# Input quarters of an attention unit rounded to two halves three steps ahead of their mixing instead of one

## The chip, the cores and the metric

One core of a Trainium2 chip runs the whole program. The metric is the device time of one execution in microseconds (us). A measurement is a median over runs.

## What is computed

The reference is a small tower: a token mixing, causal linear attention with its MLP, and a routed expert layer. The change touches the first part only, where the mixing of the input meets the attention:

```python
h = einsum('bhid,oi,od->bho', x, weighted_sum, weight)     # 16 sequences x 512 rows x 256
x0 = layernorm(h); hn = layernorm(x0) * g1 + beta1
q, k = phi((hn @ wq) @ proj), phi((hn @ wk) @ proj)        # 16 heads of 64
v = hn @ wv
# causal: kv += k v^T, ksum += k; out = q kv / (q ksum + 1e-6)
x1 = x0 + out @ wo                                         # then MLP, then the routed experts
```

## The kernel before, in words

**Precision.** Every float32 operand of a matmul is carried as two float16 tiles, a high part (rounded) and a low part (the rest), and each product is three matmuls (`three`, lines 541 to 545). So each operand needs one rounding and one subtraction. For the input the rounding to `xh` is ScalarE's (`split`, line 719) and the subtraction into `xl` is GpSimd's (line 959), each on a 128x512 tile. For the features phi(q) and phi(k), VectorE adds up `z` (line 869) and casts it to `hi` (line 874), and GpSimd makes `lo` (line 965).

**Units and steps.** The attention phase works in 32 units of 256 tokens, two for each of 16 sequences. h is 0 for the first unit of a sequence and 1 for the second. A unit has eight steps, s0 to s7 (`unit`, lines 382 to 439); each step reads out one group of four heads (`outputs`), turns an earlier group (`turn`), makes scores for a group two steps ahead (`scores`), and beside that does a piece of dense work: the eight features (n0 to n7) and four value tiles of the next unit, and the projection of the last one. Features sit at s0 (n0), s1 (n1, n2), s2 (n3), s4 (n4), s5 (n5, n6), s6 (n7). The unit after next gets its first normalisation at s0 to s2 (`mean`, `var`, `rstd`, `x0`, `normed`), and the unit three ahead is mixed at s4 to s7, one of four input quarters each (`mixed`, lines 352 to 357), with 12 matmuls for a quarter.

**Order.** One function, `run`, writes the same order of steps out for every engine, and each engine takes those steps that it has a part in, strictly in that order. What belongs to a step on an engine waits on semaphores of the others. SyncE's queue (SP) is part of this: at `split` of a quarter it waits until `xh` and `xl` of that quarter are made (lines 481, 482) and then loads the quarter of the following unit into the freed buffer (line 483, 256 KB); at `phi` of a feature it waits for `hi` and `lo` and moves them to where the scores read them: eight DMAs for a feature of q (n even), four for one of k (n odd), lines 507 to 519. The scores of s0 (line 628) wait until n7 has been moved.

**Where the change bites.** The quarter k is split at step s3 + k, so `xh` and `xl` for a mixing are made one step ahead of it. `mixed(u, k)` issues the mixing of k and then the split of k + 1. In `unit`, the split stands after `scores_split` and `sums_split` and ahead of the late feature's `phi`, so on VectorE's and GpSimd's side it stands between `kvl` (line 984) and the next `lo`. The buffers `xh` and `xl` have a place of their own for each of the four quarters, and their owner waits only for the mixing of the same quarter one unit earlier.

Of the kernel before, what the change touches and what calls it, by code (L numbers as in the profile page):

```python
# [28 lines left out]
XS = XK // 2  # L29
# [35 lines left out]
def after(u, n):  # L65

    return u[0] + (u[1] + n) // 2, (u[1] + n) % 2
# [27 lines left out]
def attention_phase(nc, io, w1_w, w2_w, mlp_loaded):  # L95
# [4 lines left out]
    with ExitStack() as ctx:  # L100
# [223 lines left out]
        def run(engine, steps):  # L324


            def step(name, *args):
                if name in steps:
                    steps[name](*args)

            def use(u, what, bank, before):


                kind, n = what
                if kind == "p":
                    step("project", after(u, -1), bank, before)
                elif kind == "f":
                    step("features", after(u, 1), n, bank, before)
                else:
                    step("values", after(u, 1), n, bank, before)  # L340

            def finish(u, what, bank):
                if what[0] == "f":
                    step("phi", after(u, 1), what[1], bank)
                elif what[0] == "p":
                    step("project_read", after(u, -1), bank)
                    step("residual", after(u, -1))

            def real(u):
                return u[0] < SEQS  # L350

            def mixed(u, k):
                step("mix", u, k)
                if k < XS - 1:
                    step("split", u, k + 1)
                else:
                    step("h", u)

            def normed(u):
                step("mean", u)  # L360
                step("centre", u)
                step("var", u)
                step("rstd", u)
                step("x0", u)
                step("normed", u)

            def dense(turn, first, last):


                slots, n = [], turn % 2  # L370
                before = {n: ("v", VALS - 2, 1), 1 - n: ("v", VALS - 1, 1)}
                for s in range(8):
                    uses = [], []
                    for place, (kind, k) in enumerate(DENSE[s]):
                        if not ((kind == "p" and first) or (kind != "p" and last)):
                            uses[place].append(((kind, k), n % 2, before[n % 2]))
                            before[n % 2] = (kind, k, 0)
                        n += 1
                    slots.append(uses)
                return slots  # L380

            def unit(u, start=False, last=False):


                i, h = u
                slots = dense(h, start, last)
                ahead, far = after(u, 2), after(u, 3)
                for s in range(8):
                    c, g = 2 * h + s // 4, s % 4
                    early, late = slots[s]  # L390

                    summed = (c, g - 2) if g >= 2 and c < CH - 1 else (c - 1, g + 2) if g < 2 and c > 0 else None

                    if g < 2:
                        quad = (i, c, g + 2)
                    elif c < CH - 1:
                        quad = (i, c + 1, g - 2)
                    else:
                        quad = None if last else (i + 1, 0, g - 2)
                    if s == 2 and real(ahead):  # L400
                        step("x0", ahead)
                        step("normed", ahead)
                    for what in early:
                        use(u, *what)
                    step("outputs", i, c, g)

                    if g >= 2:
                        step("turn", i, c, g - 2)
                    elif c > 0:
                        step("turn", i, c - 1, g + 2)  # L410
                    elif not start:
                        step("turn", i - 1, CH - 1, g + 2)
                    for what in early:
                        finish(u, *what[:2])
                    if quad is not None:
                        step("scores", *quad)
                    step("outputs_split", i, c, g)
                    if s == 1 and real(ahead):
                        step("var", ahead)
                        step("rstd", ahead)  # L420
                    for what in late:
                        use(u, *what)
                    if summed is not None:
                        step("sums", i, *summed)
                    if g in (1, 2) and c < CH - 1:
                        step("keys", i, c, g - 1)
                    if quad is not None:
                        step("scores_split", *quad)
                    if summed is not None:
                        step("sums_split", i, *summed)  # L430
                    if s == 0 and real(ahead):
                        step("mean", ahead)
                        step("centre", ahead)
                    if s == 3 and real(far):
                        step("split", far, 0)
                    if s >= 4 and real(far):
                        mixed(far, s - 4)
                    for what in late:
                        finish(u, *what[:2])

            step("split", (0, 0), 0)
            for k in range(XS):
                mixed((0, 0), k)
            normed((0, 0))
            step("split", (0, 1), 0)
            slots = dense(-1, True, False)
            for s in range(8):
                for what, bank_no, before in slots[s][0] + slots[s][1]:
                    use((0, -1), what, bank_no, before)
                    finish((0, -1), what, bank_no)  # L450
                if s < XS:
                    mixed((0, 1), s)
                elif s == 4:
                    normed((0, 1))
            step("split", (1, 0), 0)
            for k in range(XS):
                mixed((1, 0), k)
            for q in range(2):
                step("scores", 0, 0, q)
                step("scores_split", 0, 0, q)  # L460
            unit((0, 0), start=True)
            unit((0, 1))
            for i in range(1, SEQS - 1):
                unit((i, 0))
                unit((i, 1))
            unit((SEQS - 1, 0))
            unit((SEQS - 1, 1), last=True)
            step("turn", SEQS - 1, CH - 1, 2)
            step("turn", SEQS - 1, CH - 1, 3)
            step("project", (SEQS - 1, 1), LAST_BANK, ("p", 0, 1))  # L470
            step("project_read", (SEQS - 1, 1), LAST_BANK)
            step("residual", (SEQS - 1, 1))
# [4 lines left out]
        def _(sp):  # L477
# [53 lines left out]
            for k in range(XS):  # L531
                load((0, 0), k)
            run(sp, dict(split=split, phi=phi, residual=residual))
            sp.wait_ge(x1_stored, 16 * UNITS)
            sp.wait_ge(hx_stored, 16 * UNITS)
# [4 lines left out]
        def _(pe):  # L540
# [147 lines left out]
            def turn(i, c, g):  # L688
# [6 lines left out]
                for part, src in enumerate((oh, ol)):  # L695
                    for f in range(2):
                        w = 2 * part + f
                        mm = pe.transpose(pT[:, w * P:(w + 1) * P], src[:, n % 2, f * P:(f + 1) * P], ident[:, :])  # L698
                mm.then_inc(turned, 1)

            run(pe, dict(mix=mix, mean=mean, var=var, features=features, values=values, scores=scores, keys=keys,
                         outputs=outputs, sums=sums, turn=turn, project=project))

        @block.scalar
        def _(act):
# [109 lines left out]
            def sums_split(i, c, g):  # L815
# [5 lines left out]
                                     ACT.Copy).then_inc(kvh_ready, 1)  # L821

            run(act, dict(outputs=outputs, split=split, h=h, centre=centre, rstd=rstd, normed=normed, features=features, values=values,
                          scores_split=scores_split, turn=turn, outputs_split=outputs_split,
                          sums_split=sums_split))
# [1365 lines left out]
```

## Time and profile before

| what | us |
|---|---|
| median of three runs | 2545.34 |
| lowest, highest run | 2538.14, 2553.37 |
| the profiled execution, device time | 2542.18 |
| its span, first to last instruction | 2540.4 |

Of the span, TensorE is busy 2215.7 us, VectorE 1784.6, ScalarE 1524.6 and GpSimd 1467.8. The attention phase runs from about 45 to 1550 us; after it come the MLP and the routed phase, which the change does not touch and which begin when the attention phase is over. In the tables PE is TensorE, DVE VectorE, ACT ScalarE, POOL GpSimd, and SPq the queue of SyncE. The span given in a row of a timeline is start, duration, engine, line, operation, and in brackets how long the engine sat idle before it and what released it.

### The profile page before, as it was taken

Reading aid. Unit: us, or ns where it says so; the run is one execution under the profiler, and the core shown is the slowest. Engines: PE = TensorE matmul, PEld = TensorE weight load, DVE = VectorE, ACT = ScalarE, POOL = GpSimd, SP = SyncE. Lnnn points to the kernel's source line nnn. Section 1 sums busy time; section 2 is a strip of 40 time slices with the busy share of each in tenths; the row PEclk is TensorE's granted clock in tenths of the full one; section 3 lists DMA queues with packets and bytes.
Section 4 is the critical chain, followed back from the end, with each engine's and each line's share of the span. In section 5 each row is a group of like instructions: output and inputs, shape, how many; then the busy total and the mean of one; then the engine's idle time right before and its main releaser. Section 6 shows DMA issues by size and latency. Waiting matters only on the chain. (4 is left out here: it accounts for less than half of the span.)

```text
span 2540.4 us, 64867 instructions
## 1 busy us (share of the span) xinstructions
PE 2215.7 (87%) x24112; PEld 1732.1 (68%) x24112; DVE 1784.6 (70%) x3983; ACT 1524.6 (60%) x2890; POOL 1467.8 (58%) x1449
## 2 busy tenths in 40 slices
PE   3799999999989899999999986799999999994764
PEld 2577777778778777777778775466666666662653
DVE  3477777777777777777777775478788887874443
ACT  3476676676766676667667664556566565651322
POOL 1466666575666666656657654035646555556676
PEclk8899999999999999999999998899999999997897
DMA  3344444344454343434433333111212111100775
GB/s 112 97 119 113 122 123 124 104 131 122 105 132 124 100 105 102 108 99 105 110 101 104 89 87 112 40 60 45 82 43 83 45 60 52 40 22 22 166 139 72
DMA packets 323208, 236.43 MB, mean 93 GB/s; under 512 B 40345, under 2 KB 288141, under 8 KB 322896
## 3 DMA queue, kind: packets, MB, share of 16 engines
q1 hardware_dynamic: 286640, 197.30, 28.6%
q0 software_dynamic: 23808, 21.74, 4.9%
q10 hardware_dynamic: 12448, 13.24, 1.6%
q8 instruction: 195, 3.19, 0.5%
q14 instruction: 117, 0.96, 0.1%
HBM read 73.32 MB, written 82.58 MB: 61 GB/s over the span
## 5 line engine op out<-in xcount | busy, mean ns | idle before, releaser
L965 POOL TENSOR_TENSOR lo<-z,hi 128x512 f16<-128x512 f32 x256 | 306.1, 1196 | 342.8 <-DVE hi L874 328.5
L1850 POOL DMA_INDIRECT slot_dram<-xt,slot_u x256 | 267.0, 1043 | 77.4 <-issue 77.4
L543 PE MATMUL pF<-nh,qk_h 128*128 128x256 f16 x1024 | 282.7, 276 | 7.5 <-DVE nl L862 4.4
L545 PE MATMUL pF<-nl,qk_h 128*128 128x256 f16 x1024 | 282.6, 276 | 0.0
L544 PE MATMUL pF<-nh,qk_l 128*128 128x256 f16 x1024 | 282.6, 276 | 0.0
L789 ACT ACTIVATE sh<-sm 128x512 f16<-128x512 f32 x256 | 159.5, 623 | 106.3 <-DVE sm L895 106.2
L984 POOL TENSOR_TENSOR kvl<-kvacc,kvh 128x260 f16<-128x260 f32 x192 | 157.4, 820 | 77.2 <-ACT kvh L820 77.1
L869 DVE SCALAR_TENSOR_TENSOR z<-pF,z 128x512 f32<-128x512 f32 x256 | 174.9, 683 | 24.6 <-ACT z L772 22.2
L768 ACT ACTIVATE z<-pF 128x512 f32<-128x512 f32 x256 | 150.4, 587 | 69.6 <-PE pF L545 69.6
L543 PE MATMUL pM<-xh,tok_h 128*128 128x256 f16 x512 | 141.3, 276 | 53.9 <-POOL xl L959 53.3
L895 DVE TENSOR_TENSOR sm<-pS,mask 128x512 f32<-128x512 f32 x256 | 174.5, 681 | 17.2 <-PE pS L629 16.9
L977 POOL TENSOR_TENSOR ol<-on,oh 128x256 f16<-128x256 f32 x256 | 171.9, 672 | 24.4 <-ACT oh L812 24.4
L874 DVE CAST hi<-z 128x512 f16<-128x512 f32 x256 | 174.7, 682 | 8.8
L543 PE MATMUL pO<-vh,sh 128*128 128x65 f16 x1024 | 120.5, 194 | 57.1 <-issue 48.2
L796 ACT ACTIVATE ot<-pT 128x512 f16<-128x512 f16 x256 | 149.3, 583 | 33.1 <-PE pT L698 32.9
L628 PE MATMUL pS<-qdh,ks 128*128 128x128 f16 x1024 | 143.6, 221 | 29.1 <-DMA ks<-lo 28.2
L772 ACT ACTIVATE z<-z 128x512 f32<-128x512 f32 x256 | 161.4, 630 | 8.1
L812 ACT ACTIVATE oh<-on 128x256 f16<-128x256 f32 x256 | 105.5, 412 | 96.9 <-DVE on L927 94.0
L1838 POOL TENSOR_TENSOR xt<-xn,xt 128x512 f16<-128x512 f32 x32 | 40.0, 1269 | 208.5 <-ACT xt L1521 208.5
L2100 POOL DMA_INDIRECT out_rows<-yb,xg x80 | 126.7, 1583 | 58.3 <-ACT yb L2045 33.0
L919 DVE TENSOR_SCALAR dn<-pO 128x4 f32<-128x4 f32 x256 | 39.9, 156 | 170.0 <-PE pO L545 169.7
L959 POOL TENSOR_TENSOR xl<-w_w,xh 128x512 f16<-128x512 f32 x128 | 147.9, 1158 | 18.1 <-ACT xh L719 18.1
(298 smaller groups left out, 8494.2 us busy)
## 6 DMA issues: line engine op xcount, KB each, us to landing
w_w<-in_x SPq DMA_DIRECT2D x128, 256.0 KB, 3.0
qdh<-hi SPq DMA_DIRECT2D x512, 64.0 KB, 2.1
qdl<-lo SPq DMA_DIRECT2D x512, 64.0 KB, 2.1
ks<-hi SPq DMA_DIRECT2D x256, 64.0 KB, 2.1
ks<-lo SPq DMA_DIRECT2D x256, 64.0 KB, 2.1
slot_dram<-blank ACTq DMA_DIRECT2D x8, 1360.0 KB, 7.1
xg<-slot_dram SPq DMA_DIRECT2D x40, 272.0 KB, 3.2
x_dram<-x SPq DMA_DIRECT2D x32, 256.0 KB, 2.4
```

Of the source, the lines that this page charges most:

```text
L543: pe.matmul(out, wh, mh, start=first, stop=False, skip_group_check=True)
L544: pe.matmul(out, wl, mh, start=False, stop=False, skip_group_check=True)
L545: return pe.matmul(out, wh, ml, start=False, stop=last, skip_group_check=True)
L772: nc.scalar.activation(z[:, s, :, :], z[:, s, :, :], ACT.Exp, scale=-1.0, bias=-math.log(PHI_DOWN)).then_inc(e_ready, 1)
L789: nc.scalar.activation(sh[:, q, :, :], sm[:, n % 2, :, :], ACT.Copy).then_inc(sh_ready, 1)
L869: nc.vector.scalar_tensor_tensor(z[:, s, :, :], pF[bank_no][:, :].rearrange("p (b n) -> p b n", b=2), 0.0, z[:, s, :, :], ALU.max, ALU.add ...
L874: nc.vector.tensor_copy(hi[:, n % MOVES, :, :], z[:, s, :, :]).then_inc(fh_ready, 1)
L895: nc.vector.tensor_tensor(sm[:, n % 2, :, :], pS[:, :].rearrange("p (a b) -> p a b", b=P), mask[:, :].unsqueeze(1).broadcast_to([P, 4, P]) ...
L965: nc.gpsimd.tensor_tensor(lo[:, n % 2, :, :], z[:, units(w, FEATS, n) % ZS, :, :], hi[:, n % MOVES, :, :], ALU.subtract).then_inc(fl_ready, 1)
L977: nc.gpsimd.tensor_tensor(ol[:, n % 2, :], on[:, n % 2, :, :].rearrange("p a b -> p (a b)"), oh[:, n % 2, :], ALU.subtract).then_inc(ol_re ...
L984: nc.gpsimd.tensor_tensor(kvl[:, heads, :], kvacc[:, heads, :], kvh[:, heads, :], ALU.subtract).then_inc(kvl_ready, 1)
L1850: nc.gpsimd.indirect_dma_start(io["slot_dram"], bass.IndirectOffsetOnAxis(slot_u[:, i % XT, c, k:k + 1], 0), xt[:, i % XT, c, :], None, bo ...
```

## The change

All four splits of a unit move: in the steady units from s3, s4, s5, s6 to s1, s2, s3, s4. The mixings stay at s4 to s7. For the first units, which are written out by hand, the splits of unit (0, 1) are issued together ahead of its mixing; those of (0, 0) and (1, 0) keep their order.

```diff
             def mixed(u, k):
                 step("mix", u, k)
-                if k < XS - 1:
-                    step("split", u, k + 1)
-                else:
+                if k == XS - 1:
                     step("h", u)
...
-                    if s == 3 and real(far):
-                        step("split", far, 0)
+                    if 1 <= s <= XS and real(far):
+                        step("split", far, s - 1)
                     if s >= 4 and real(far):
                         mixed(far, s - 4)
...
-            step("split", (0, 0), 0)
             for k in range(XS):
+                step("split", (0, 0), k)
                 mixed((0, 0), k)
             normed((0, 0))
-            step("split", (0, 1), 0)
+            for k in range(XS):
+                step("split", (0, 1), k)
...
-            step("split", (1, 0), 0)
             for k in range(XS):
+                step("split", (1, 0), k)
                 mixed((1, 0), k)
```

## Rows read from the trace of the kernel before

**Rows 1.** The page: span and busy time of each engine.
```profile
span 2540.4 us, 64867 instructions
PE 2215.7 (87%) x24112; PEld 1732.1 (68%) x24112; DVE 1784.6 (70%) x3983; ACT 1524.6 (60%) x2890; POOL 1467.8 (58%) x1449
```

**Rows 2.** TensorE's waits, 200 to 1450 us: total, times, longest.
```profile
PE pO L543 <- issue: 41.1, 27, 1.8
PE pM L543 <- POOL xl L959: 33.6, 55, 1.9
PE pS L628 <- DMA ks<-lo: 23.4, 24, 2.6
```

**Rows 3.** Timeline of ScalarE: the first and last `h` of 28 steady units.
```profile
157.12 0.60 ACT L725 ACTIVATE hT<-pM 128x512 f32<-128x512 f32 x1
...
1451.28 0.60 ACT L725 ACTIVATE hT<-pM 128x512 f32<-128x512 f32 x1
```

**Rows 4.** Timeline of TensorE: mixing at s7, outputs at s4, scores at s0 twice.
```profile
753.51 0.27 PE L543 MATMUL pM<-xh,tok_h 128*128 128x256 f16 x1 [1.19 <-POOL xl L959]
...
782.26 0.19 PE L543 MATMUL pO<-vh,sh 128*128 128x65 f16 x1 [1.63 <-issue]
...
1408.22 0.22 PE L628 MATMUL pS<-qdh,ks 128*128 128x128 f16 x1 [1.60 <-DMA ks<-lo]
...
1497.85 0.27 PE L628 MATMUL pS<-qdh,ks 128*128 128x128 f16 x1 [2.48 <-DMA ks<-lo]
```

**Rows 5.** Timeline of VectorE: casts of n4, with loads behind them and without.
```profile
1387.21 0.43 DVE L874 CAST hi<-z 128x512 f16<-128x512 f32 x1
...
1479.33 0.43 DVE L874 CAST hi<-z 128x512 f16<-128x512 f32 x1
```

**Rows 6.** Timeline of SyncE's queue from n4's first move to n7's last.
```profile
1387.66 0.59 SPq L507 DMA_DIRECT2D qdh<-hi  x1
...
1397.12 0.54 SPq L483 DMA_DIRECT2D w_w<-in_x  x1
1397.70 0.59 SPq L507 DMA_DIRECT2D qdh<-hi  x1
...
1400.29 1.63 SPq L516 DMA_DIRECT2D qdl<-lo  x1
...
1405.22 1.25 SPq L519 DMA_DIRECT2D ks<-lo  x2
```

**Rows 7.** The same queue at s5 of a unit where it runs dry.
```profile
470.03 1.25 SPq L519 DMA_DIRECT2D ks<-lo  x2
472.20 0.33 SPq L483 DMA_DIRECT2D w_w<-in_x  x1
```

**Rows 8.** Timeline of ScalarE at s1: h = 1 (720 us), h = 0 (767 us).
```profile
721.16 0.40 ACT L820 ACTIVATE kvh<-kvacc 128x260 f16<-128x260 f32 x1
...
767.51 0.61 ACT L789 ACTIVATE sh<-sm 128x512 f16<-128x512 f32 x1
771.90 0.91 ACT L754 ACTIVATE nh<-w_w,b 128x256 f16<-128x256 f32 x2 [3.78 <-DVE w_w L856]
```

**Rows 9.** Timeline of GpSimd: s1 of h = 1, s1 of h = 0, s5.
```profile
721.64 0.88 POOL L984 TENSOR_TENSOR kvl<-kvacc,kvh 128x260 f16<-128x260 f32 x1 [1.79 <-ACT kvh L820]
...
770.05 1.47 POOL L965 TENSOR_TENSOR lo<-z,hi 128x512 f16<-128x512 f32 x1 [3.35 <-DVE hi L874]
...
792.82 1.15 POOL L959 TENSOR_TENSOR xl<-w_w,xh 128x512 f16<-128x512 f32 x1
```

**Rows 10.** Timeline of VectorE: cast n2 (h = 1, h = 0), n6; `nl`, `sl`.
```profile
722.61 0.43 DVE L874 CAST hi<-z 128x512 f16<-128x512 f32 x1
...
769.48 0.43 DVE L874 CAST hi<-z 128x512 f16<-128x512 f32 x1
...
772.51 0.88 DVE L862 SCALAR_TENSOR_TENSOR nl<-w_w,b,nh 128x256 f16<-128x256 f32 x2 [0.31 <-ACT nh L754]
...
781.37 0.68 DVE L902 TENSOR_TENSOR sl<-sm,sh 128x512 f16<-128x512 f32 x1
...
791.29 1.02 DVE L902 TENSOR_TENSOR sl<-sm,sh 128x512 f16<-128x512 f32 x1
...
792.95 1.30 DVE L874 CAST hi<-z 128x512 f16<-128x512 f32 x1
```

**Rows 11.** Timeline of TensorE: a mixing of unit (0, 1).
```profile
77.70 0.27 PE L543 MATMUL pM<-xh,tok_h 128*128 128x256 f16 x1 [2.73 <-POOL xl L959]
```

## The prediction

> **What bounds the kernel now.** I read the page first [rows 1]: TensorE is busy for 87% of the span, which invites the thought that any stall taken from it is gained. TensorE's waits come next [rows 2]. In 27 units (200 to 1450 us) it waits 33.6 us for `xl`, the wait that the change aims at: 1.24 us a unit, mostly at the mixing of s7, as in [rows 4], 753.51. But it also waits 23.4 us for the last move of `ks` (0.87 a unit, at the scores of s0) and 41.1 us at the outputs of s4, where the row names no releaser; there `sl`, made by VectorE just before, ends the wait [rows 4, 10]. A wait that stands right behind the removed one takes back what it gives, so the question is what sets the time of the scores of s0.
>
> The steady unit lasts (1451.28 - 157.12) / 28 = 46.2 us [rows 3]. I cut it at two events: the cast of n4 at s4, and the scores of s0.
>
> Second part, n4's cast to s0's scores. In the unit of 1387 us the cast ends at 1387.64 and SyncE's queue begins n4's moves at 1387.66 [rows 5, 6]. From there it issues back to back: 24 moves (n4 to n7: 8 + 4 + 8 + 4), each 0.59 to 0.65 us from start to start, and two loads of input quarters, each 0.58 us to the next start (1397.12 to 1397.70). Its last move ends at 1406.47 and the scores start 1.75 later, having waited 1.60 us [rows 4, 6]. So the queue, not TensorE, ends this part: 20.58 us. A few issues take 1.0 to 2.0 us instead of 0.61 (1.63 at 1400.29), about 1.3 us extra in a unit; I see no link with the loads. The trace holds its own experiment: in the unit of 1479 us there is neither load nor mixing; cast end 1479.76, scores 1497.85, so 18.09 us, and TensorE waits even longer, 2.48 us [rows 4, 5]. With no mixing at all in the way, the scores still wait for the queue.
>
> First part, s0's scores to n4's cast, about 25.6 us. TensorE makes `mean`, then ScalarE works without a gap to the end of s1, then VectorE almost without one (0.31 us before `nl` [rows 10]) from 768.15 to `sl` at 781.37, which releases the outputs of s4 [rows 4]; from those come `on`, `z` and the cast of n4. So in this part a delay of VectorE in s1 to s3 goes straight into the unit.
>
> **The change, part by part.** Nothing is added or removed: in each of 29 units (u = 0 to 28, those with a unit three ahead) four roundings, four subtractions and four loads move two steps forward.
>
> *TensorE's wait for `xl`*: gone. Worth 1.24 us on TensorE, 0 by itself, as the scores of s0 are held by the queue; TensorE arrives earlier and waits longer there.
>
> *Queue, second part.* Of the two loads between n4's and n7's moves, that of s4 stays (it now follows the split of quarter 3) and that of s5 goes: -0.58 us. That of s6 stood behind n7's moves and frees nothing. Also, in 9 of 28 units I found the queue idle, 0.33 to 0.92 us and 7.5 us in all, mostly as in [rows 7]: n5's moves are out at 471.28, the load waits for `xl` until 472.20. That wait goes with the load, -0.25 a unit. Could n6's cast hold the queue instead? It starts at 792.95 and takes 1.30 us because `xl` of s5 started at 792.82 [rows 9, 10]; without that it takes 0.43, so n6 is ready 0.87 earlier, enough. Sum: -0.83.
>
> *Queue, first part.* The loads at s1 and s2 go ahead of n2's and n3's moves, each waiting for its `xl`. n2 and n3 are first read by the scores of s6, four steps on, and the queue has idle stretches at s2 and s3; what is queued behind the load, n2's moves and the stores, has that slack: 0. If the slack were gone it would be 2 x 0.58.
>
> *ScalarE.* Rounding at s1 falls in its idle time: in h = 0 it has nothing from 768.12 to 771.90 (3.78 idle), in h = 1 from 721.56 on [rows 8]. At s2 it delays `vh` by 0.52 us, and `vh` is still ready ahead of VectorE's `vl`: 0; uncovered, it would cost 0.52.
>
> *GpSimd against VectorE*, the cost of the change. VectorE's cast of a feature takes 0.43 us, but 1.30 when it starts 0.13 us into a GpSimd operation that lasts 1.15 [rows 9, 10]: it gets through 0.27 after that operation's end. Today n2's cast is undisturbed in both kinds of unit, 0.43 [rows 10]. After the change a subtraction of 1.15 us stands before it at s1. In h = 0, `sh` ends at 768.12, the rounding at about 768.65, `xl` runs about 768.72 to 769.88, and the cast of 769.48 takes (769.88 - 769.48) + 0.28 = 0.68: +0.26. In h = 1, `kvh` ends at 721.56, the rounding at 722.1, GpSimd's `kvl` at 722.52 [rows 8, 9]; `xl` starts then, 0.1 us ahead of the cast of 722.61, so this takes about 1.31: +0.88. Mean +0.57. This lies on VectorE's chain, so it counts in full. Its bounds: 0 if the cast slips through, 0.88 in both kinds. At s2 the second `xl` pushes `lo` of n3 and `ol` back by 1.15, so that `ol` ends about 0.2 us into `sl` of 781.37. `sl` takes 0.68 undisturbed and 1.02 at worst [rows 10]; I take +0.08, bounds 0 and 0.34. `ol` itself is turned two steps later: 0. Sum of the first part: +0.65.
>
> The Trainium skill (SBUF — State Buffer, section "Who interferes with whom") speaks of this: GpSimd and such a VectorE operation use one pair of ports, and whichever issues first has it for the whole instruction. [Rows 9, 10] agree, with 1.30 against 0.43 us.
>
> *The prologue.* Unit (0, 1) is mixed between dense pieces, and one mixing waits 2.73 us for `xl`, behind `lo` tiles that wait for moves [rows 11]. Splits in one piece ahead of it end that; ScalarE and GpSimd are idle there. What follows moves up with it: -2.5 us, between -2.73 and 0.
>
> **Sum.** (-0.83 + 0.65) x 29 = -5.2, and -2.5: -7.7 us. The profiled execution took 2542.18 us, 1.8 above its span, so 2534.5 us. It lies 3.2 below the median of the runs, 2545.34, whose extremes are 15 us apart. About 0.5% (12.7 us) is what a measurement of this kernel can tell from no change.
>
> **The rivals.**
> *A: TensorE is the bound after all.* Then 1.24 x 29 + 2.7 = 38.7 us are gained, 2503.5. For it: 87% busy, and units without any wait at s0 (3 of 27). Against it: the unit of 1479 us.
> *B: the cast is not hit.* In h = 1 cast and `xl` are only 0.1 us apart. If the cast comes first, it costs nothing there, and the first part is worth 0.13 + 0.08: (-0.83 + 0.21) x 29 - 2.5 = -20.5 us, 2521.7. By the page named above, with its lock for the one that issues first, this race decides; the trace bears out both orders, a cast of 0.43 and one of 1.30.
> *C: slower, by VectorE's chain.* If in h = 0 too the cast finds `xl` just started, and `sl` finds `ol` whole, the first part grows by 0.88 + 0.34 = 1.22, while the queue gives only its 0.58: +0.64 x 29 = 18.6, with no gain in the prologue 2560.8. It decides where cast wait and `sl` together pass the queue's gain of 0.58 to 0.83. Against it: in h = 0 the gap before the cast is wide.
> *D: the splits don't run early.* They would have to wait for the load or the buffer; but the load comes a whole unit ahead and the buffer has been read at the same quarter's mixing one unit ago. No chance given.
>
> **Chances.** Forecast 0.56, A 0.08, B 0.20, C 0.16. A and B are faster by over 0.5%, and 0.04 of the forecast's; C is slower. Faster 0.32, same 0.52, slower 0.16. The range takes in B and most of C, and stops short of A: 2510 to 2556.
>
> **What would show it.** Right: TensorE's wait for `xl` near 0 in steady units, its wait for `ks` up from 0.87 to about 1.9 us a unit; n2's cast near 0.68 (h = 0) and 1.3 (h = 1) instead of 0.43; n6's cast 0.43 instead of 1.30; one load between n4's and n7's moves; second part about 0.8 us shorter, first part 0.6 longer. Wrong: the wait at s0 unchanged while units get shorter (A), n2's cast at 0.43 in h = 1 (B), or outputs of s4 waiting over 2.5 us (C).

## The result, and the profile after

The changed kernel takes 2527.12 us (median of nine runs, 2524.55 to 2533.73) against 2545.34 us (nine runs, 2538.14 to 2553.37): a ratio of 0.993, 95% interval 0.9914 to 0.9947. It is faster by 0.7%, 18 us, where 7.7 had been forecast (the profiled executions, 2542.18 and 2524.87 us, are 17.3 apart). The range, 2510 to 2556, held it, but that range spans gain and loss alike; the likeliest outcome, no change beyond 0.5%, did not come.

The page of the changed kernel, for [rows 1]:

```profile
span 2523.1 us, 64867 instructions
PE 2212.0 (88%) x24112; PEld 1729.1 (69%) x24112; DVE 1784.6 (71%) x3983; ACT 1529.7 (61%) x2890; POOL 1469.6 (58%) x1449
```

Nobody does less work. What changed is who waits. Its list of TensorE's waits from 200 to 1450 us, for [rows 2] (total, times, longest; attention lines are one less than before):

```profile
PE pO L542 <- issue: 41.4, 27, 1.6
PE pS L627 <- DMA ks<-lo: 25.9, 26, 1.9
PE pT L637 <- ACT ot L795: 16.6, 27, 0.9
PE pO L542 <- DVE sl L901: 8.8, 27, 0.7
```

The wait for `xl`, 33.6 us before, has left the list. The wait for the last move of `ks` has stayed (23.4, now 25.9), and two waits of s2 to s4 have come or grown. ScalarE's `h`, for [rows 3], gives the steady unit as (1434.68 - 155.21) / 28 = 45.7 us, 0.5 less than before:

```profile
155.21 0.58 ACT L724 ACTIVATE hT<-pM 128x512 f32<-128x512 f32 x1
...
1434.68 0.58 ACT L724 ACTIVATE hT<-pM 128x512 f32<-128x512 f32 x1
```

Now the two parts of a unit. Timeline of VectorE, for [rows 10]: n2's cast with h = 0, n6's cast, n2's cast with h = 1:

```profile
760.56 0.68 DVE L873 CAST hi<-z 128x512 f16<-128x512 f32 x1
...
784.30 0.43 DVE L873 CAST hi<-z 128x512 f16<-128x512 f32 x1
...
806.82 1.30 DVE L873 CAST hi<-z 128x512 f16<-128x512 f32 x1
```

And GpSimd's `xl` at s1 in the same two units, for [rows 9]:

```profile
759.80 1.16 POOL L958 TENSOR_TENSOR xl<-w_w,xh 128x512 f16<-128x512 f32 x1 [2.01 <-ACT xh L718]
...
806.68 1.15 POOL L958 TENSOR_TENSOR xl<-w_w,xh 128x512 f16<-128x512 f32 x1
```

The casts of n2 rise from 0.43 to 0.68 and 1.30 us, as priced; in h = 1 `xl` did win by 0.14 us (806.68 against 806.82). n6's cast fell from 1.30 to 0.43. SyncE's queue from n4's first move to n7's last, for [rows 6], and the scores that wait for it, for [rows 4]:

```profile
1372.72 0.59 SPq L506 DMA_DIRECT2D qdh<-hi  x1
...
1378.49 0.54 SPq L482 DMA_DIRECT2D w_w<-in_x  x1
...
1385.55 1.42 SPq L515 DMA_DIRECT2D qdl<-lo  x1
...
1388.97 1.25 SPq L518 DMA_DIRECT2D ks<-lo  x2
```

```profile
1391.95 0.22 PE L627 MATMUL pS<-qdh,ks 128*128 128x128 f16 x1 [1.26 <-DMA ks<-lo]
```

One load is left in the stretch, and the scores still wait for the queue.

For all kernels below I cut the 28 units between the scores of s0 of the second and the thirtieth unit in the prediction's two parts, by the casts of n4 and the scores of s0 in each kernel's one trace, and took means. The second part, its loads, stalls and dry time and the wait for `ks` are means over the 28 second parts that end at the second to twenty-ninth scores of s0, as the one that ends at the thirtieth has no load; so the two parts do not add up to the unit exactly. "Queue stalls" is what the issues of the stretch take beyond 0.65 us each; "dry" is the queue's idle time in it.

| us | first part, h = 0 / h = 1 | second part | loads in it | queue stalls | dry | wait for `ks` | unit |
|---|---|---|---|---|---|---|---|
| before | 25.60 / 26.04 | 20.40 | 2 | 1.31 | 0.27 | 0.86 | 46.19 |
| changed | 25.76 / 26.87 | 19.38 | 1 | 1.31 | 0.06 | 0.97 | 45.66 |
| e1 | 26.40 / 27.15 | 20.22 | 2 | 1.28 | 0.05 | 1.81 | 46.87 |
| e2 | 25.80 / 26.32 | 19.69 | 0 | 1.33 | 0.87 | 0.24 | 45.73 |
| e3 | 25.74 / 25.98 | 19.51 | 1 | 1.25 | 0.25 | 0.94 | 45.34 |
| e4 | 25.72 / 27.02 | 18.88 | 0 | 1.32 | 0.18 | 0.50 | 45.22 |
| e5 | 25.47 / 26.01 | 19.37 | 0 | 1.18 | 0.88 | 0.79 | 45.11 |
| e6 | 27.78 / 28.40 | 21.72 | 4 | 1.41 | 0.07 | 2.90 | 49.56 |
| e7 | 26.45 / 26.80 | 19.40 | 1 | 1.32 | 0.08 | 0.99 | 46.02 |
| e8 | 25.64 / 26.16 | 18.83 | 0 | 1.21 | 0.25 | 0.44 | 44.74 |

The means of the first part hold units with a lowered granted clock, most of them 1.6 to 2 us longer (see the last section): nine in e1, 25 in e6, three in e3, one or two or none in the others. The medians, h = 0 / h = 1, are 25.47 / 25.94 before, 25.57 / 26.83 for the changed kernel, 25.33 / 25.95 for e3 and for e5, and 25.62 / 26.06 for e8.

### The profile page after: what moved, and what is told of

It is laid out like the page before. It is cut to its first block and busy times, and to the rows that moved or that the text cites. A ratio compares the mean times of both kernels' runs of the same rounds, so it can differ in the third digit from the quotient of the medians.

```text
span 2523.1 us, 64867 instructions
## 1 busy us (share of the span) xinstructions
PE 2212.0 (88%) x24112; PEld 1729.1 (69%) x24112; DVE 1784.6 (71%) x3983; ACT 1529.7 (61%) x2890; POOL 1469.6 (58%) x1449
## 5 line engine op out<-in xcount | busy, mean ns | idle before, releaser
L970 POOL TENSOR_TENSOR sl<-sm,sh 128x512 f16<-128x512 f32 x128 | 148.6, 1161 | 11.2 <-ACT sh L788 11.1
```

## The experiments

The question: did the gain come from SyncE's queue, as I had argued, or from the wait that the change takes from TensorE? In all of these kernels but e7 the load of a quarter is a step of its own, `step("load", far, k)`, so that it can stand elsewhere in the queue than the split.

**e1: rounding early, loads where they were.**

```diff
+LOADS = {3: (0,), 4: (1,), 5: (2,), 6: (3,)}
...
-            run(sp, dict(split=split, phi=phi, residual=residual))
+            run(sp, dict(load=split, phi=phi, residual=residual))
```

> The changed kernel, with the four loads of SyncE's queue back at s3 to s6, each one behind another feature's moves, while the roundings and subtractions stay at s1 to s4. Queue theory (the gain came from the load that left the stretch between n4's and n7's moves): two loads in that stretch again, second part of the unit +0.6 to 0.9 us against the changed kernel, so about 2527 + 28 x 0.6 to 0.9 = 2544 to 2552 us, no faster than before. Rival (TensorE's wait for xl was the gain): the loads do not matter, 2527 us.

Measured: 2557.87 us, ratio 1.0056 (1.0035 to 1.0077). Slower than the kernel before, though no wait of TensorE for `xl` is left in its list from 200 to 1450 us, whose first rows show where the time is:

```profile
PE pS L636 <- DMA ks<-lo: 46.3, 27, 2.9
PE pO L551 <- issue: 39.6, 26, 1.6
```

Of the removed 33.6 us, 22.9 have come back as waits for the queue (46.3 against 23.4). So the early rounding alone gains nothing. The second part is 0.84 us longer than in the changed kernel (0.76 without the one that ends in a wait of 4.31 us, see the last section), inside the 0.6 to 0.9 expected. The time went past the expectation by the first part, +0.45: in nine of the 28 units TensorE's granted clock is low behind the wait at s0, and their first parts are 1.6 to 2.6 us longer, on which more below.

**e2: rounding late as before, loads at s7.**

```diff
                         mixed(far, s - 4)
+                    if s == 7 and real(far):
+                        for k in range(XS):
+                            step("load", far, k)
```

> The kernel before, with its roundings and subtractions where they were (s3 to s6), and the four loads together at s7, behind n7's moves. Queue theory: no load between n4's and n7's moves, second part down from 20.4 us until TensorE, which still waits for xl, becomes its bound at about 19.5; first part unchanged, as n2's cast is not hit: about 2545 - 29 x 0.8 = 2522 us. Rival (TensorE's wait for xl was the gain): that wait is still there, so 2545 us as before.

Measured: 2534.09 us, ratio 0.9949 (0.9931 to 0.9968). Moving nothing but the loads gains; the rival is out. But it gains 10.5 us, not 23. Its waits:

```profile
PE pM L551 <- POOL xl L967: 32.3, 56, 1.2
...
PE pS L636 <- DMA ks<-lo: 6.0, 7, 1.5
```

Here TensorE has become the bound: it waits for `xl` as before (32.3 us) and hardly for the queue. The second part stopped at 19.69, close to the 19.5 given. The first part and the prologue lost some (the scores of s0 of the second unit come at 163.4 us, against 160.0 before; 3.0 us of this were there at the first unit's s0), which I had not expected and for which I have no cause.

**e3: no split at s1.**

```diff
+SPLITS = {2: (0,), 3: (1,), 4: (2, 3)}
+LOADS = {2: (0,), 3: (1,), 4: (2,), 7: (3,)}
```

> The changed kernel with the splits at s2, s3, s4, s4 instead of s1, s2, s3, s4, and the loads at s2, s3, s4 and s7, so that one load stays between n4's and n7's moves as in the changed kernel. Cast theory (xl at s1 holds back n2's cast by 0.8 us in h = 1 and 0.25 in h = 0, on VectorE's chain): first part down by 0.55 us, n2's cast 0.43 us again, about 2527 - 29 x 0.55 = 2511 us. Rival (VectorE's chain has slack, the cast costs nothing): 2527 us.

Measured: 2515.36 us, ratio 0.988 (0.9849 to 0.991), 12 us below the changed kernel, where 16 were expected and the rival gave 0. VectorE's timeline in a unit with h = 1:

```profile
797.13 0.43 DVE L882 CAST hi<-z 128x512 f16<-128x512 f32 x1
```

n2's cast is undisturbed again, and the first part of h = 1 falls by 0.89 us, from 26.87 to 25.98, which is the cast's 0.87. In h = 0 the mean stays, 25.74 against 25.76, but 11 of the 14 units are at 25.31 to 25.60 and the median falls by 0.24, from 25.57 to 25.33, again the cast's 0.25. The mean is held up by three units of 26.98 to 27.34, which begin at 1195.64, 1287.97 and 1380.41 us behind waits of 1.5 to 2.2 us; the granted clock is 0.57 to 0.59 in their first 4 us. Those three cost some 5 us, about what is missing from the 16 expected.

**e4: the changed kernel with all loads at s7** (`LOADS = {7: (0, 1, 2, 3)}`).

> The changed kernel with all four loads at s7, behind n7's moves. Queue theory: the last load leaves the stretch, second part -0.55 us against the changed kernel (19.4 to 18.8; TensorE would arrive at about 18.4): 2527 - 28 x 0.55 = 2512 us. Rival (TensorE bound): 2527 us.

Measured: 2515.51 us, ratio 0.9887 (0.9856 to 0.9918). The second part is 0.50 us shorter for one load of 0.58, and the run landed 3.5 us from the expected time. It was measured again beside e8:

> e4 once more beside e8, so that the two are compared on one chip: 2515 us, second part 18.9 us, first part 26.4 us with n2's cast hit.

2513.55 us, ratio 0.9882 (0.9856 to 0.9907): the same.

Before, e1, e2 and e4 make a square. With the loads where they were, early rounding costs 13 us (2544.6 to 2557.9). With the loads out of the way it gains 19 (2534.1 to 2515.5). TensorE's wait for `xl` is worth something only when the queue does not stand behind it.

**e5: e3 and e4 together** (`SPLITS = {2: (0,), 3: (1,), 4: (2, 3)}`, `LOADS = {7: (0, 1, 2, 3)}`).

> Both improvements of the last batch together: splits at s2, s3, s4, s4 (n2's cast undisturbed) and all four loads at s7 (none between n4's and n7's moves). If the two terms belong to different parts of the unit they add up: first part 25.9 as in e3, second part 18.9 as in e4, a unit of 44.8 us, about 2527 - 12 - 12 = 2502 us. Rival (both runs took the same slack out of one wait): no more than one of them, 2515 us.

Measured: 2515.63 us, ratio 0.9879 (0.9863 to 0.9896): the rival's time, and for a while it looked like a floor at 2515. But the trace gives two other reasons. About 5 us of the shortfall lie behind the attention phase, in code that is the same: from the last unit's scores of s0 to the end it takes 1005.3 us, against 1001.1 in the changed kernel and 1000.8 and 1000.6 in e3 and e4. The cause of that is open. The other, a unit of 45.11 us instead of 44.8, is the queue's dry time of 0.88 us. The queue and GpSimd at s4 and s5:

```profile
728.61 1.82 SPq L518 DMA_DIRECT2D ks<-hi  x2
730.64 1.24 SPq L527 DMA_DIRECT2D ks<-lo  x2
732.64 0.59 SPq L515 DMA_DIRECT2D qdh<-hi  x1
```

```profile
727.04 2.46 POOL L967 TENSOR_TENSOR xl<-w_w,xh 128x512 f16<-128x512 f32 x2
729.46 1.15 POOL L973 TENSOR_TENSOR lo<-z,hi 128x512 f16<-128x512 f32 x1
```

Two subtractions in a row at s4 push `lo` of n5 to 730.61. The queue has n5's high moves out at 730.43 and must wait for it, then again from 731.88 to 732.64 for n6. The emptied queue was starved by the placement of the splits: e4, with the splits as changed, has a dry time of 0.18.

**e6: four loads in the stretch** (`LOADS = {4: (0, 1, 2, 3)}`, splits as changed).

> The changed kernel with all four loads of the queue at s4, so four of them between n4's and n7's moves instead of one. Queue theory: three more loads of 0.58 us each, second part from 19.4 to 21.1 us, TensorE's wait at s0 up by as much, 2527 + 28 x 1.74 = 2576 us, more if the granted clock falls after the longer waits as it did in e1. Rival (the queue has slack, loads are hidden): 2527 us.

Measured: 2634.41 us, ratio 1.0329 (1.0299 to 1.0359). Twice the expected loss. The second part is 2.34 us longer (1.74 expected; 2.20 without the first one, which ends in a wait of 7.3 us). The rest, about 1.8 a unit, is in the first part, at a mean granted clock of 0.96 and 0.95 in the windows from 200 and 700 us, where the changed kernel has 1.00. TensorE's wait for `ks` from 200 to 1450 us was up to 5.2 us:

```profile
PE pS L636 <- DMA ks<-lo: 69.9, 25, 5.2
```

Not all of this is the queue's. In seven units the last move of `ks` lands 4.0 to 6.7 us after its issue instead of 2.1, some 18 us in all, and in each ScalarE's own queue had issued a transfer of 1360 KB (`slot_dram<-blank`, once in each of the first eight sequences) 0.2 to 0.7 us ahead of it. In the changed kernel that transfer is issued behind the last move, and every last move of the 28 units lands within 2.2 us.

**e7: the split of s1 behind n2's cast and `lo`.**

```diff
                     for what in late:
                         finish(u, *what[:2])
+                    if s == 1 and real(far):
+                        step("split", far, 0)
```

> The changed kernel with quarter 0's split still at s1, but behind n2's cast and lo instead of ahead of them; loads as in the changed kernel. If it is only the cast that is hit: cast 0.43 us again, first part -0.55, 2527 - 16 = 2511 us. What I expect instead is that GpSimd's xl now runs from the end of n2's lo and holds up the second of VectorE's two tn operations (line 856 of before, 1.2 us when it meets a GpSimd operation and 0.47 when not): +0.7 in both kinds of unit in place of 0.8 and 0.25, so about the same as the changed kernel or up to 6 us more, 2527 to 2533 us.

Measured: 2535.11 us, ratio 0.9948 (0.9931 to 0.9966), 8 us over the changed kernel. The two were not run together, and by the ratios, 0.9948 and 0.993, the distance is some 5 us with intervals that overlap; the traces give a unit of 46.02 against 45.66 us. VectorE and GpSimd at s1, h = 0:

```profile
765.96 0.43 DVE L877 CAST hi<-z 128x512 f16<-128x512 f32 x1
...
767.09 2.49 DVE L859 SCALAR_TENSOR_TENSOR w_w<-x,g,r 128x256 f32<-128x256 f32 x2
```

```profile
766.53 1.47 POOL L968 TENSOR_TENSOR lo<-z,hi 128x512 f16<-128x512 f32 x1 [3.36 <-DVE hi L877]
767.96 1.33 POOL L962 TENSOR_TENSOR xl<-w_w,xh 128x512 f16<-128x512 f32 x1
```

The cast is free, and the two `tn` operations take 2.49 us where they took 1.59 in the changed kernel (761.94 us): both now meet a GpSimd operation. The cost sits in s1's VectorE chain, wherever in it the subtraction stands.

**e8: quarter 0 at s7 of the unit before, none at s1, one at a step, no load in the stretch.**

```diff
+SPLITS = {2: (1,), 3: (2,), 4: (3,)}
+LOADS = {1: (0,), 7: (1, 2, 3)}
...
                         mixed(far, s - 4)
+                    if s == 7 and real(after(u, 4)):
+                        step("split", after(u, 4), 0)
...
                 mixed((1, 0), k)
+            step("split", (1, 1), 0)
```

> Quarter 0 is split at s7 of the unit before, where GpSimd and VectorE are both idle, quarters 1 to 3 at s2, s3, s4 as in the changed kernel; load 0 at s1, loads 1 to 3 at s7. No xl meets n2's cast and none stands in s5, and no load lies between n4's and n7's moves. Queue and cast theory: second part 18.9 us as in e4, first part 25.9 us as in e3, a unit of 44.8 us against 45.7 of the changed kernel, 2527 - 28 x 0.9 = 2502 us. Rival (something else holds the unit at 45.1 to 45.3 us, as e3, e4 and e5 all ended there): 2515 us.

Measured: 2499.03 us (2496.77 to 2500.35), ratio 0.9822 (0.9802 to 0.9842), 45 us below the kernel before, 14.5 below e4 beside it, and the fastest of all. Both parts came out as expected (18.83 and 25.90 on average), so 2515 was no floor. GpSimd and VectorE at s7 and s0, where `xl` now fits into the gap ahead of n0's cast:

```profile
780.97 1.15 POOL L970 TENSOR_TENSOR xl<-w_w,xh 128x512 f16<-128x512 f32 x1
```

```profile
782.79 0.43 DVE L885 CAST hi<-z 128x512 f16<-128x512 f32 x1
```

Its waits:

```profile
PE pO L554 <- issue: 42.8, 28, 1.6
PE pS L639 <- DMA ks<-lo: 11.8, 18, 1.7
PE pO L554 <- DVE sl L913: 10.0, 28, 1.3
```

What is left is the wait at s4's outputs for VectorE's chain, much the same in every kernel (38.6 to 42.8 us from 200 to 1450 us).

## Why the prediction was right, and where its sizes were off

The step-by-step argument held. *The bound* of the second part is the queue: e1, e2, e4 and e6 move only loads, and the second part follows their number (0 loads 18.88, 1 load 19.38, 2 loads 20.22, 4 loads 21.72, all with early splits; in the last two the `slot_dram` transfer has its share). The unit without loads, used as the trace's own experiment [rows 4, 5], had said so. *TensorE's wait* was worth 0 by itself: in e1 it is gone, and the second part is 0.18 us shorter than before, with 0.22 us less dry time. Rival A is out.

*The cast.* Predicted 0.68 and about 1.31, measured 0.68 and 1.30; e3 takes them away and gets back 0.89 us of h = 1 and, in the median, 0.24 of h = 0. The trace decided rival B's race by 0.14 us. By the Trainium skill (SBUF — State Buffer, "Who interferes with whom") the one that issues first keeps the ports for its whole instruction. e7 agrees, where the two `tn` operations, each with two inputs in SBUF, take 2.49 us beside GpSimd's `lo` and `xl`.

*The sizes.* Two terms of nearly equal size and opposite sign were taken from each other, so small errors weigh much. The second part was given -0.83 and came to -1.02: the load about 0.5 (0.58 priced), the dry time 0.21 (0.25 priced), and 0.30 more between the end of the last issue and the scores, 2.02 us before and 1.72 after. I had taken one unit's 1.75 for it [rows 6, 4] without looking at the others; five of the 28 before were at 2.8 to 3.5, as the last move of `ks` there took up to 3.9 us to land instead of 2.1. None did so in the changed kernel. It is not the number of loads in the stretch: e2, with none, has 1.90 and landings of up to 3.2 us. What makes these landings long in some units is open, so this 0.30 was no term of mine and its gain is unexplained. The first part was given +0.65 and came to +0.50. In the usual units it was nearly as given, 0.27 and 0.89 (25.30 to 25.57 and 25.94 to 26.83), so `sl` cost about 0.02 where I had 0.08. But the mean before held eleven longer ones. Eight of them stand behind a wait for `ks` of at most 0.5 us, as if a short wait were in part given back in the first part, which no run here shows by itself; one, 26.96, has the lowered clock. The prediction treated the two parts as independent. Together -0.53 a unit instead of -0.18: over 28 units 14.9 us instead of 5.

*The ends.* The prologue was given -2.5; the scores of s0 of the second unit come 1.8 us earlier. From the scores of s0 of the thirtieth unit to those of the last it took 1.5 us less, in code that is the same, which no term of mine had. With 1.0 us lost after that, this is the 17.3 us between the spans, to 0.1. One trace cannot size such ends: e4 and its repetition, the same kernel, differ by 1.3 us at the second unit's scores.

*Two slips.* "From 0.87 to about 1.9" for the wait for `ks` did not follow from my own terms. They give 0.87 + 1.24 - 0.83 = 1.28; it was 0.97. And the range was said to take in most of C, while C's own time, 2560.8, lies above its end of 2556.

*The chances.* Faster had 0.32. The forecast was placed by a sum whose two terms I trusted to 0.1 us, while 0.2 us a unit was the distance to the bound of 0.5%.

## What to carry to other kernels

Before a wait is worth removing, find what holds the next event behind it: here a DMA queue that issues at 0.65 us apiece. Taking loads of 0.58 us out of its way gained 10 us and more, while taking away the visible stall of 33.6 us alone gained nothing. A piece of work can be moved for free only to where no engine's chain is tight, and both halves must be looked at: its own engine, and the engine that shares something with it. When an improvement has two parts, run each alone and both; e1 shows that the part after which the change is named costs time by itself.

## What was not expected

**The granted clock after a wait.** In e1 the scores of one s0 start at 162.20 us after 4.31 us of waiting. Windows around it (us; busy time of PE, PEld, DVE, ACT, POOL; granted clock, DMA share, GB/s):

```profile
158.00:162.00 4.00, 0.00 (x0) 0.00 (x0) 1.53 (x4) 1.13 (x3) 1.78 (x2) 0.85 0.90 255
162.00:166.00 4.00, 3.80 (x24) 3.10 (x25) 1.47 (x3) 0.94 (x2) 1.32 (x2) 0.50 0.98 282
166.00:170.00 4.00, 4.00 (x50) 3.38 (x49) 1.48 (x5) 2.64 (x5) 0.47 (x1) 0.80 0.24 56
```

From 162 to 166 us the clock is 0.50, the lower of its two levels (1.2 instead of 2.4 GHz), and that first part took 29.44 us instead of 26.83. In the unit of 395.8 us, after 2.15 us of waiting, the window from 396 to 400 shows 0.57 and the first part 27.24 instead of 25.56. So a wait at s0 can cost twice, and in e6, where the clock is low behind 25 of 28 of these waits, that is most of the loss beyond what its loads account for. It does not take so long a wait: in e7 the clock is 0.57 in the 4 us behind one of 1.26 us, and the changed kernel has one such unit, behind 1.52 us. In e1 a wait of 2.73 us was not followed by it; what decides is open.

The 4.31 us themselves are not the queue's alone. ScalarE's queue issued its large transfer 0.28 us ahead of the last move of `ks`, the second of the two in this row, which landed 4.06 us after its issue:

```profile
157.24 1.25 SPq L527 DMA_DIRECT2D ks<-lo  x2
...
157.61 0.60 ACTq L720 DMA_DIRECT2D slot_dram<-blank  x1
```

In the traces here every last move issued less than 1 us behind that transfer, eight in all, took 4.0 to 6.7 us to land, and no other took over 3.9. No run moved the transfer away, so that it is the cause is argued and not shown.

**The queue's long issues.** The 1.3 us of stalls a unit in the stretch hardly depend on the loads in it (1.18 to 1.33 with none, 1.41 with four). I did not find their cause, and nothing here tried to remove them.
